# The first stage of a fused token, attention and mixture-of-experts kernel: order of loads, of the readout bias and of the first transposes, and which tokens a partition holds

## The chip, the cores and the metric

The kernel runs on one core of a Trainium2 chip. The metric is the device time of one execution in microseconds (us), the median of several runs. Everything is computed in float32; where a product needs precision on TensorE, each operand is split into a high and a low part (`_hi`, `_lo`, type fp32r) and three matmuls are added up.

## The reference, cut to what matters

```python
# x: 16 x 256 x 256 (batch, tokens, features); token 0 of each batch is the readout token
readout, other = X[:, :1, :], X[:, 1:, :]
h = gelu(other @ W[:d] + readout @ W[d:] + b)                    # token stage, exact gelu
def attn(x):                                                     # 16 heads of 64
    q, k, v = split(x @ Wq.T), split(x @ Wk.T), split(x @ Wv.T)
    e = exp(s - max(s)), s = q k^T / 8
    return merge(e / (sum(e) + 1e-10) @ v) @ Wo.T + bo
def moe(x):                                                      # 8 experts, best 2 per row
    routed = sum over the best two experts of p_e * (silu(x @ w1[e]) @ w2[e])
    shared = sigmoid(x @ gate_w) * ((silu(gate) * up) @ shared_down)
    return routed + shared
h = h + attn(layernorm(h))
h = h + moe(layernorm(h))                                        # out: 16 x 255 x 256
```

## The kernel before

The 4096 rows of x (16 batches of 256 tokens) are worked on in 8 groups of two batches, 512 rows each. A group lies in SBUF as 128 partitions by 4 row tiles (`GT` = 4) by 256 features; tile t of partition p is token p of the half-batch t. The result of the token stage, `resid`, keeps this layout to the end of the program, and the stores to `out` undo it.

The program has two blocks. Between them all engines meet at a barrier.

`token_phase` is the first block. For each group g, TensorE does in this order: the 12 matmuls of the token product into `tok_ps` (helper lines L70 to L72; `group`), the 8 transposes of the next group's input (`transpose_x`, L198, out to `xT_ps`), 8 transposes that prepare two banks of the attention weights (`weights`, L242), and the 8 transposes that turn the result back to rows (`rows`, L255, out to `h_ps`). ScalarE does four gelus (L287), then the high parts of the next input (`x_hi`, L275) and of the weights (L296). VectorE does the low parts (`x_lo`, L313; weights, L324) and then copies `h_ps` to `resid` (L328). After four groups VectorE has the layernorm statistics of the first group and GpSimd its reciprocal deviation; in group 5 VectorE writes the normalised rows `z` (L339).

Ahead of group 0 TensorE transposes the 16 readout rows (`ro`, L206), transposes the first input tile, and multiplies the readout rows by the lower half of the token weight (L213, the readout bias). VectorE copies the transposed readout rows (L301), splits the token weight (`tokw_lo`, L303), adds the bias column (`rbias`, L307), and only then makes the low parts of the first input tile (L313). ScalarE splits the token weight first (`tokw_hi`, L268) and then the input tile. All loads of this block are issued on SyncE's queue, in the order readout rows, token weight, two input tiles, the four attention weights, and then six more input tiles, each of which waits for the transposes that free its buffer.

`main_phase` is the second block: attention over the 8 groups with the router of the group before mixed in, then the expert tiles (71 of them), then the sums and the stores. Its first work on TensorE is `transpose_z` of group 0 (L676, out to `pT_ps`), on ScalarE a load of the exp table (L1032) and `z_hi` (L1057), on VectorE some constants, two pairs of statistics and `z_lo` (L1274); then come the first q and k projections (L70 to L72 into `proj_ps`). Every engine's order is written out by hand, and semaphores connect them. In `store_group` each group is stored by three DMAs (L615, L617, L619) once its last addition (L1470) is done.

Of the kernel before, what the change touches and what calls it, by code (L numbers as in the profile page):

```python
# [62 lines left out]
def f32(ap):  # L63

    return ap.bitcast(F32)
# [9 lines left out]
def build(nc, x, tok_w, tok_b, wq, wk, wv, wo, bo, router_w, w1, w2, gate_up, down, gate_w, out):  # L75
    x_rows = x.rearrange("b (h p) d -> p (b h) d", p=P)
    with ExitStack() as ctx:
# [15 lines left out]
                                                                  "rstd_ready", "z_ready")]  # L93
        qkv_at = nc.sbuf_base
# [4 lines left out]
        token_phase(nc, x, x_rows, tok_w, tok_b, wq, wk, wv, wo, resid, z, norm_sems, ident, half_neg,  # L99
                    qkv_parts, [wo_both[:, n] for n in range(2)])  # L100
        main_phase(nc, bo, router_w, gate_w, w1, w2, gate_up, down, out, resid, z, norm_sems, ident, half_neg,
# [3 lines left out]
def token_phase(nc, x, x_rows, tok_w, tok_b, wq, wk, wv, wo, resid, z, norm_sems, ident, half_neg,  # L105
                qkv_parts, wo_parts):


    with ExitStack() as ctx:
# [25 lines left out]
        s_ro, s_tokw, s_bcol = sem("ro_in"), sem("tokw_in"), sem("bcol_in")  # L135
# [14 lines left out]
        s_st, s_mv, s_var, s_rstd, s_z = norm_sems  # L150

# [50 lines left out]
        def _(pe):  # L202
            pe.wait_ge(s_const, IDENT_SET)
            pe.wait_ge(s_ro, 16)
# [3 lines left out]
            transpose_x(pe, 0)  # L208
            pe.wait_ge(s_readout, ROT_READY)
            pe.wait_ge(s_tokw, 16)  # L210
            for e in range(DC):
                for c in range(DC):
                    m = pe.matmul(h_ps[1][:, e * B:(e + 1) * B], tokw[:, DC + c, e * P:(e + 1) * P], roT[:, c, :],  # L213
                                  start=c == 0, stop=c == DC - 1)
            m.then_inc(s_readout, 1)

            def group(g, last):
# [6 lines left out]
                for e in range(DC):  # L224
# [4 lines left out]
                    m.then_inc(s_tok, 1)  # L229
                if not last:  # L230
                    transpose_x(pe, g + 1)

            def weights(g):

                for j in range(per_group):
# [7 lines left out]
                    m.then_inc(s_w, 1)  # L243

# [14 lines left out]
            for g in range(GROUPS):  # L259
                group(g, g == GROUPS - 1)  # L260
                weights(g)
                rows(g)

        @block.scalar
        def _(act):
            act.dma_start(bcol[:], tok_b.rearrange("(c p) -> p c", p=P), allow_slow_non_contiguous=True).then_inc(s_bcol, 16)
            act.wait_ge(s_tokw, 16)
            act.activation(tokw_hi[:], tokw[:, 0:DC, :], ACT.Copy).then_inc(s_tw, 1)  # L268

# [6 lines left out]

            x_hi(0)
            for g in range(GROUPS):
# [12 lines left out]
                for j in range(per_group):  # L291
# [7 lines left out]
        def _(dve):  # L299
            dve.wait_ge(s_readout, ROT_IN_PSUM)  # L300
            dve.tensor_copy(roT[:], h_ps[0][:, 0:DC * B].rearrange("p (c b) -> p c b", c=DC)).then_inc(s_readout, 1)  # L301
            dve.wait_ge(s_tw, TOKW_HI)
            dve.tensor_tensor(tokw_lo[:], tokw[:, 0:DC, :], f32(tokw_hi[:]), ALU.subtract).then_inc(s_tw, 1)  # L303
# [5 lines left out]

            def x_lo(g):  # L310
# [35 lines left out]
def main_phase(nc, bo, router_w, gate_w, w1, w2, gate_up, down, out, resid, z, norm_sems, ident, half_neg, qkv_parts,  # L346
# [11 lines left out]
    with ExitStack() as ctx:  # L358
# [308 lines left out]
        def _(pe):  # L667
# [252 lines left out]
            for c in range(DC):  # L920
                transpose_z(0, c)
# [939 lines left out]
```

## Time and profile before

| | us |
|---|---|
| median of 3 runs | 1057.47 (1057.09 to 1058.63) |
| the profiled execution's own time | 1057.78 |
| span of its profile | 1056.0 |
| PE busy | 1010.3 (96%) |
| DVE busy | 741.5 (70%) |
| ACT busy | 660.6 (63%) |
| POOL busy | 510.8 (48%) |

PE is TensorE's matmul side and PEld its weight loads, DVE is VectorE, ACT is ScalarE, POOL is GpSimd, SP is SyncE; a q behind the name (SPq) is the issue of DMAs. The span runs from the first to the last recorded instruction or transfer; 1.8 us of the execution lie outside it. PE's busy share is that of the whole span: it holds for the attention and the experts, and not for the first ten microseconds, the passage between the two blocks and the end.

### The profile page before, as it was taken

Reading aid. Unit: us, or ns where it says so; the run is one execution under the profiler, and the core shown is the slowest. Engines: PE = TensorE matmul, PEld = TensorE weight load, DVE = VectorE, ACT = ScalarE, POOL = GpSimd, SP = SyncE. Lnnn points to the kernel's source line nnn. Section 1 sums busy time; section 2 is a strip of 40 time slices with the busy share of each in tenths; the row PEclk is TensorE's granted clock in tenths of the full one; section 3 lists DMA queues with packets and bytes.
Section 4 is the critical chain, followed back from the end, with each engine's and each line's share of the span. In section 5 each row is a group of like instructions: output and inputs, shape, how many; then the busy total and the mean of one; then the engine's idle time right before and its main releaser. Section 6 shows DMA issues by size and latency. Waiting matters only on the chain.

```text
span 1056.0 us, 23175 instructions
## 1 busy us (share of the span) xinstructions
PE 1010.3 (96%) x8042; PEld 875.0 (83%) x8042; DVE 741.5 (70%) x1912; ACT 660.6 (63%) x1939; POOL 510.8 (48%) x557
## 2 busy tenths in 40 slices
PE   6979999999999999999999999999998889999996
PEld 5867888888888888888888888888876779998985
DVE  3757775787688578767857876775783766666677
ACT  4657884787578478757847775784783555554541
POOL 0016543557365455736645573664444486444420
PEclk9999999999999999999999999999999999999998
DMA  8210000001000000100000010000021834444479
GB/s 269 71 46 2 1 2 1 21 1 42 21 1 22 21 21 2 42 21 2 21 22 21 1 42 21 1 22 21 22 70 62 265 89 139 133 142 122 127 225 318
DMA packets 47496, 65.91 MB, mean 62 GB/s; under 512 B 7992, under 2 KB 39480, under 8 KB 47384
## 3 DMA queue, kind: packets, MB, share of 16 engines
q1 hardware_dynamic: 40056, 44.50, 13.5%
q0 software_dynamic: 7056, 19.93, 5.6%
q8 instruction: 68, 1.11, 0.4%
q14 instruction: 44, 0.36, 0.1%
q10 hardware_dynamic: 272, 0.00, 0.0%
HBM read 36.09 MB, written 28.33 MB: 61 GB/s over the span
## 4 chain that ended last, share of the span: by engine, by line
PE 73%; DVE 9%; DMA 4%; ACT 4%; issue 2%; SPq 2%; POOL 0%; DVEq 0%; ACTq 0%; POOLq 0%
PE proj_ps L70 12%; PE proj_ps L72 12%; PE proj_ps L71 12%; PE pT_ps L731 10%; PE proj_ps L744 10%; PE s_ps L713 8%; DMA back<-expert_out_rows 2%; ACT prob L1041 2%; DMA xg<-expert_in_rows 2%; PE s_ps L70 2%; PE s_ps L72 2%; PE s_ps L71 2%; PE s_ps L963 1%; PE pT_ps L984 1%; DVE z L1389 1%
## 5 line engine op out<-in xcount | busy, mean ns | idle before, releaser
L1041 ACT ACTIVATE prob<-s_ps,nmax 128x255 f32<-128x255 f32 x512 | 237.8, 479 | 140.5 <-DVE nmax L1263 139.5
L1720 POOL TENSOR_SCALAR prob<-prob,rinv 128x255 f32<-128x255 f32 x128 | 138.4, 1081 | 258.5 <-DVE rinv L1281 258.0
L1263 DVE TENSOR_REDUCE nmax<-s_ps 128x2 f32<-128x510 f32 x256 | 159.2, 679 | 23.2 <-PE s_ps L713 22.7
L731 PEld LDWEIGHTS pT_ps<-ident,prob 128*128 128x128 f32 x1024 | 114.6, 140 | 37.3 <-issue 29.1
L731 PE MATMUL pT_ps<-ident,prob 128*128 128x128 f32 x1024 | 136.9, 276 | 3.6 <-ACT probT L1067 3.3
L744 PE MATMUL proj_ps<-probT,v 128*64 128x256 f32 x1024 | 125.1, 386 | 2.1 <-DVE probT L1288 2.1
L1722 POOL TENSOR_SCALAR prob<-prob,rinv 128x255 f32<-128x255 f32 x128 | 119.2, 931 | 0.0
L1270 DVE TENSOR_TENSOR qk_space<-proj_ps,qk_space 128x512 fp32r<-128x512 f32 x128 | 87.6, 685 | 38.2 <-ACT qk_space L1053 37.8
L1048 ACT ACTIVATE prob<-prob,rinv 128x255 f32<-128x255 f32 x128 | 67.3, 526 | 66.7 <-DVE rinv L1281 66.5
L713 PE MATMUL s_ps<-qk_space 64*128 64x256 f32 x1536 | 108.3, 287 | 0.4 <-DVE qk_space L1270 0.3
L1041 ACT ACTIVATION_READ_ACCUMULATOR prob<-s_ps,nmax 128x1 f32 x512 | 108.5, 212 | 0.0
L713 PEld LDWEIGHTS s_ps<-qk_space 64*128 64x128 f32 x1536 | 95.3, 186 | 8.0 <-issue 2.3
L1811 POOL DMA_INDIRECT expert_out_rows<-yg,y_at x71 | 68.1, 959 | 68.3 <-DVE yg L1626 63.3
L744 PEld LDWEIGHTS proj_ps<-probT,v 128*64 128x64 f32 x1024 | 67.8, 136 | 38.8 <-issue 2.1
L1053 ACT ACTIVATE qk_space<-proj_ps 128x512 fp32r<-128x512 f32 x128 | 79.0, 618 | 14.8 <-PE proj_ps L72 14.6
L1288 DVE COPY probT<-pT_ps 128x512 f32<-128x512 f32 x128 | 87.0, 679 | 0.0
L70 PE MATMUL proj_ps<-wv_hi,zT_lo 128*128 128x256 f32 x256 | 77.6, 303 | 2.3 <-DVE qk_space L1270 2.2
L1067 ACT ACTIVATE probT<-pT_ps 128x512 f32<-128x512 f32 x128 | 79.0, 618 | 0.8 <-PE pT_ps L731 0.8
L1744 POOL DMA_INDIRECT expert_in_rows<-z,slot_now x64 | 64.3, 1005 | 25.5 <-issue 17.4
L1293 DVE TENSOR_TENSOR oT_lo<-proj_ps,oT_hi 128x512 fp32r<-128x512 f32 x64 | 44.2, 691 | 45.8 <-ACT oT_hi L1072 45.8
L71 PE MATMUL proj_ps<-wo_both,oT_hi 128*128 128x256 f32 x256 | 72.5, 283 | 0.0
L70 PE MATMUL proj_ps<-wo_both,oT_lo 128*128 128x256 f32 x256 | 72.5, 283 | 0.0
(261 smaller groups left out, 2697.5 us busy)
## 6 DMA issues: line engine op xcount, KB each, us to landing
xg<-expert_in_rows SPq DMA_DIRECT2D x71, 130.0 KB
back<-expert_out_rows SPq DMA_DIRECT2D x6, 1024.0 KB, 21.6
xin<-in_x_dram SPq DMA_DIRECT2D x8, 512.0 KB, 4.6
z_rows<-z SPq DMA_DIRECT2D x8, 512.0 KB, 3.2
z<-z_rows SPq DMA_DIRECT2D x8, 512.0 KB, 4.4
expert_in_rows<-bo_row SPq DMA_DIRECT2D x16, 128.0 KB
raw_up<-in_L_ffn_w_dram SPq DMA_DIRECT2D x8, 256.0 KB, 5.4
raw_down<-in_L_ffn_w_dram SPq DMA_DIRECT2D x8, 256.0 KB, 6.1
```

Of the source, the lines that this page charges most:

```text
L70: pe.matmul(out, wl, xh, start=start, stop=False, skip_group_check=True)
L71: pe.matmul(out, wh, xl, start=False, stop=False, skip_group_check=True)
L72: return pe.matmul(out, wh, xh, start=False, stop=stop, skip_group_check=True)
L713: m = pe.matmul(s_ps[b][h][:, qt * N:(qt + 1) * N], a[part, rows], k[part, keys], start=n == 0, stop=n == 2)
L731: m = pe.transpose(pT_ps[h][:, o:o + P], prob[u_par(u)][:, h, qt, kt * P:(kt + 1) * P], ident[:])
L744: m = pe.matmul(o_ps[h * DH:(h + 1) * DH, b * N:(b + 1) * N], vt[:, 2 * b + kt, col:col + DH], probT[b][:, h, kt, :], start=kt == 0, stop= ...
L1041: m = act.activation(prob[u_par(u)][:, h, qt, 1:N], s_ps[b][h][:, qt * N + 1:(qt + 1) * N], ACT.Exp, bias=nmax[b][:, n:n + 1], accum_out=r ...
L1263: dve.tensor_reduce(nmax[b][:, 2 * h:2 * h + 2], s_ps[b][h][:].rearrange("p (q k) -> p q k", q=2)[:, :, 1:N], AX_X, ALU.max, negate=True). ...
L1270: dve.tensor_tensor(lo[:], proj_ps[j % 2][:], f32(hi[:]), ALU.subtract).then_inc(s_qkl, 1)
L1288: dve.tensor_copy(probT[i % 2][:, 1, :, :], pT_ps[1][:].rearrange("p (k q) -> p k q", k=2)).then_inc(s_pB, 1)
L1720: pool.tensor_scalar(prob[k][:, 0, 1, 1:N], prob[k][:, 0, 1, 1:N], rinv[k][:, 1:2], None, ALU.mult).then_inc(s_nA1, 1)
L1722: pool.tensor_scalar(prob[k][:, 1, 0, 1:N], prob[k][:, 1, 0, 1:N], rinv[k][:, 2:3], None, ALU.mult).then_inc(s_nB, 1)
```

## The change

Five things change, all in the first block but the last part of the fifth.

1. The first input tile is the first load on SyncE's queue, then come the readout rows, the token weight in two halves with a semaphore each, and the second input tile. The later input tiles stand between the attention weights, and each still waits for the transposes that free its buffer; the loads of wk, wv and wo now stand behind such waits.
2. TensorE transposes the first input tile before the readout rows, and multiplies for the readout bias after group 0's token product.
3. VectorE makes the low parts of the weight and of the first tile before it copies the readout rows and adds the bias.
4. The transposes of `z` for group 0 and the high and low parts of them are made at the end of the first block, by `transpose_z` in group 7 ahead of `rows`, into the banks of `xT_ps`; the second block begins with the projections.
5. Partition p holds the tokens 2p and 2p+1 of each batch in place of p and p+128. A load or store of a partition then touches runs of two rows (2 KB) in place of one (1 KB). The three stores of a group have other shapes: rows of partitions 16 to 127, of 1 to 15, and the one row (token 1) of partition 0.

```diff
-    x_rows = x.rearrange("b (h p) d -> p (b h) d", p=P)
+    x_rows = x.rearrange("b (p h) d -> p b (h d)", p=P)
@@ block.sync, first block
+            def load_x(g):
+                if g >= 2:
+                    sp.wait_ge(s_xT_ps, DC * (g - 1))
+                sp.dma_start(xin[g % 2][:].rearrange("p (b h) d -> p b (h d)", b=2),
+                             x_rows[:, 2 * g:2 * g + 2, :]).then_inc(x_in[g % 2], 16)
+
+            load_x(0)
             sp.dma_start(ro[:], x[:, 0, :]).then_inc(s_ro, 16)
-            sp.dma_start(tokw[:], tok_w.rearrange("(c p) e -> p c e", p=P)).then_inc(s_tokw, 16)
-            sp.dma_start(xin[0][:], x_rows[:, 0:GT, :]).then_inc(x_in[0], 16)
-            sp.dma_start(xin[1][:], x_rows[:, GT:2 * GT, :]).then_inc(x_in[1], 16)
+            for n in range(2):
+                sp.dma_start(tokw[:, n * DC:(n + 1) * DC, :],
+                             tok_w[n * D:(n + 1) * D, :].rearrange("(c p) e -> p c e", p=P)).then_inc(s_tokw[n], 16)
+            load_x(1)
             for i, w in enumerate((wq, wk, wv)):
                 sp.dma_start(raw[i][:], w.rearrange("(r p) d -> p r d", p=P)).then_inc(s_raw[i], 16)
+                load_x(2 + i)
             sp.dma_start(raw_o[:], wo.rearrange("(c p) i -> p c i", p=P)).then_inc(s_raw[3], 16)
-            for g in range(2, GROUPS):
-                sp.wait_ge(s_xT_ps, DC * (g - 1))
-                sp.dma_start(xin[g % 2][:], x_rows[:, GT * g:GT * g + GT, :]).then_inc(x_in[g % 2], 16)
+            for g in range(5, GROUPS):
+                load_x(g)
@@ block.tensor, in group(g, last)
+                if g == 0:
+                    readout_bias()
                 if not last:
                     transpose_x(pe, g + 1)
...
+            def transpose_z():
+                pe.wait_ge(s_z, GT)
+                for c in range(DC):
+                    for t in range(GT):
+                        m = pe.transpose(xT_ps[c][:, t * P:(t + 1) * P], z[:, t, c * P:(c + 1) * P], ident[:])
+                    m.then_inc(s_zt, 1)
...
                 weights(g)
+                if g == GROUPS - 1:
+                    transpose_z()
                 rows(g)
@@ block.scalar, at its end
+            for c in range(DC):
+                act.wait_ge(s_zt, c + 1)
+                act.activation(zT_hi[:, c, :], xT_ps[c][:], ACT.Copy).then_inc(s_zh, 1)
@@ block.vector, ahead of the copies of h_ps
+                if g == GROUPS - 1:
+                    for c in range(DC):
+                        dve.wait_ge(s_zh, c + 1)
+                        dve.tensor_tensor(zT_lo[:, c, :], xT_ps[c][:], f32(zT_hi[:, c, :]), ALU.subtract).then_inc(s_zl, 1)
@@ store_group, second block
-                rows = resid[:, GT * g:GT * g + GT, :].rearrange("p (b h) d -> p b h d", h=2)
-                sp.dma_start(out[2 * g:2 * g + 2, HEAD - 1:P - 1, :].rearrange("b p d -> p b d"),
-                             rows[HEAD:P, :, 0, :]).then_inc(s_out, 16)
-                sp.dma_start(out[2 * g:2 * g + 2, 0:HEAD - 1, :].rearrange("b p d -> p b d"),
-                             rows[1:HEAD, :, 0, :]).then_inc(s_out, 16)
-                sp.dma_start(out[2 * g:2 * g + 2, P - 1:N - 1, :].rearrange("b p d -> p b d"),
-                             rows[:, :, 1, :]).then_inc(s_out, 16)
+                rows = resid[:, GT * g:GT * g + GT, :].rearrange("p (b h) d -> p b (h d)", h=2)
+                both = out[2 * g:2 * g + 2, 1:N - 1, :].rearrange("b (p h) d -> p b (h d)", h=2)
+                sp.dma_start(both[HEAD - 1:P - 1], rows[HEAD:P]).then_inc(s_out, 16)
+                sp.dma_start(both[0:HEAD - 1], rows[1:HEAD]).then_inc(s_out, 16)
+                sp.dma_start(out[2 * g:2 * g + 2, 0:1, :].rearrange("b p d -> p b d"),
+                             rows[0:1, :, D:2 * D]).then_inc(s_out, 16)
@@ block.tensor, block.scalar and block.vector, second block: the first lines go
-            for c in range(DC):
-                transpose_z(0, c)
...
-            for c in range(DC):
-                z_hi(0, c)
...
-            for c in range(DC):
-                z_lo(0, c)
```

The next piece is TensorE's order at the start of the program, as a difference (line, operation, out<-in, shape, count).

```order
-L206 MATMUL h_ps<-ident,ro 128x16 x2
-L198 MATMUL xT_ps<-ident,xin 128x128 x8
-L213 MATMUL h_ps<-roT,tokw 128x16 x4
+L210 MATMUL xT_ps<-ident,xin 128x128 x8
+L219 MATMUL h_ps<-ident,ro 128x16 x2
 L70 MATMUL tok_ps<-xT_hi,tokw_lo 128x512
 L71 MATMUL tok_ps<-xT_lo,tokw_hi 128x512
```

The four bias matmuls (L213, now L227) have left their place ahead of the token product; they stand behind its twelfth matmul, ahead of the transposes of tile 1. VectorE's order at the same place, before:

```order
L301 COPY roT<-h_ps 128x32 [waits readout_bias_step]
L303 TENSOR_TENSOR tokw_lo<-tokw,tokw_hi 128x512 [waits tokw_step]
L307 TENSOR_SCALAR rbias<-h_ps,bcol 128x16 [waits bcol_in,readout_bias_step]
L307 TENSOR_SCALAR rbias<-h_ps,bcol 128x16
L313 TENSOR_TENSOR xT_lo<-xT_ps,xT_hi 128x512 [waits xT_hi_ready] x4
```

And of the change:

```order
L333 TENSOR_TENSOR tokw_lo<-tokw,tokw_hi 128x512 [waits tokw_step]
L330 TENSOR_TENSOR xT_lo<-xT_ps,xT_hi 128x512 [waits xT_hi_ready] x2
L336 COPY roT<-h_ps 128x32 [waits readout_bias_step]
L340 TENSOR_SCALAR rbias<-h_ps,bcol 128x16 [waits bcol_in,readout_bias_step]
L340 TENSOR_SCALAR rbias<-h_ps,bcol 128x16
L330 TENSOR_TENSOR xT_lo<-xT_ps,xT_hi 128x512 [waits xT_hi_ready] x2
```

The first tile's two low parts no longer stand behind the bias. VectorE's order across the end of the first block (L109 and L111 are the barrier), before:

```order
L324 SCALAR_TENSOR_TENSOR wo_both<-w_ps,wo_both 128x512 [waits w_hi_ready] x2
L328 COPY resid<-h_ps 128x512 [waits h_in_psum] x2
L109 UNCONDITIONAL_BRANCH
```

And of the change:

```order
L350 SCALAR_TENSOR_TENSOR wo_both<-w_ps,wo_both 128x512 [waits w_hi_ready] x2
L355 TENSOR_TENSOR zT_lo<-xT_ps,zT_hi 128x512 [waits zT_hi2] x2
L358 COPY resid<-h_ps 128x512 [waits h_in_psum] x2
L111 UNCONDITIONAL_BRANCH
```

The two low parts of `zT` have moved in front of the last two copies of the block; the same pair stood behind the statistics of the second block.

## Rows read from the trace of the kernel before

**Rows 1.** Stretches: us, busy time per engine, granted clock, DMA share, GB/s.

```profile
0.00:62.00 62.00, 50.79 (x298) 43.32 (x298) 34.12 (x64) 32.41 (x67) 2.00 (x9) 1.00 0.45 145
90.00:854.00 764.00, 753.06 (x6192) 639.04 (x6188) 558.18 (x1453) 519.88 (x1580) 406.85 (x439) 1.00 0.09 30
1012.00:1056.00 44.00, 34.29 (x197) 30.12 (x196) 33.96 (x50) 11.70 (x21) 3.62 (x4) 0.91 0.96 298
```

**Rows 2.** Timeline, first 13 us: start, us busy, engine, line, what, [idle before].

```profile
1.26 0.41 SPq L171 DMA_DIRECT2D tokw<-in_L_tok_W_dram  x1
1.72 0.50 SPq L172 DMA_DIRECT2D xin<-in_x_dram  x1
5.38 0.63 ACT L268 ACTIVATE tokw_hi<-tokw 128x512 fp32r<-128x512 f32 x1 [2.81 <-DMA tokw<-in_L_tok_W_dram]
6.88 1.97 PE L198 MATMUL xT_ps<-ident,xin 128*128 128x128 f32 x8 [3.97 <-DMA xin<-in_x_dram]
8.64 1.73 PE L213 MATMUL h_ps<-roT,tokw 128*128 128x16 f32 x8
8.89 0.60 ACT L275 ACTIVATE xT_hi<-xT_ps 128x512 fp32r<-128x512 f32 x1 [0.26 <-PE xT_ps L198]
10.41 0.38 DVE L307 TENSOR_SCALAR rbias<-h_ps,bcol 128x16 f32<-128x16 f32 x2 [3.68 <-PE h_ps L213]
10.70 1.28 DVE L313 TENSOR_TENSOR xT_lo<-xT_ps,xT_hi 128x512 fp32r<-128x512 f32 x2
12.04 0.80 PE L70 MATMUL tok_ps<-xT_hi,tokw_lo 128*128 128x512 f32 x1 [1.66 <-DVE xT_lo L313]
```

**Rows 3.** Timeline, group 0 to group 1, and group 7's first matmul.

```profile
15.05 1.28 ACT L287 ACT_TABLE_LOAD   x1 [5.57 <-PE tok_ps L72]
16.35 0.84 ACT L287 ACTIVATE hT<-tok_ps,rbias 128x256 f32<-128x256 f32 x2
16.90 0.49 PE L72 MATMUL tok_ps<-xT_hi,tokw_hi 128*128 128x512 f32 x1
17.42 0.84 ACT L287 ACTIVATE hT<-tok_ps,rbias 128x256 f32<-128x256 f32 x2 [0.24 <-PE tok_ps L72]
20.12 0.50 PE L70 MATMUL tok_ps<-xT_hi,tokw_lo 128*128 128x512 f32 x1
54.83 0.50 PE L70 MATMUL tok_ps<-xT_hi,tokw_lo 128*128 128x512 f32 x1
```

**Rows 4.** DMA issues: what, count, KB each, median us to landing.

```profile
raw_v<-in_L_attn_Wv_dram SPq DMA_DIRECT2D x1, 1024.0 KB, 11.9
tokw<-in_L_tok_W_dram SPq DMA_DIRECT2D x1, 512.0 KB, 4.1
```

**Rows 5.** Timeline, end of the first block and start of the second.

```profile
57.69 1.03 PE L242 MATMUL w_ps<-ident,raw_o 128*128 128x128 f32 x8
58.78 1.09 PE L255 MATMUL h_ps<-ident,hT 128*128 128x128 f32 x8
59.25 1.29 DVE L324 SCALAR_TENSOR_TENSOR wo_both<-w_ps,wo_both 128x512 fp32r<-128x512 f32 x2 [2.09 <-ACT wo_both L296]
60.45 1.28 DVE L328 COPY resid<-h_ps 128x512 f32<-128x512 f32 x2
62.20 1.06 PE L676 MATMUL pT_ps<-ident,z 128*128 128x128 f32 x8 [2.33 <-PEq L109]
64.09 1.29 DVE L1274 TENSOR_TENSOR zT_lo<-pT_ps,zT_hi 128x512 fp32r<-128x512 f32 x2 [0.52 <-ACT zT_hi L1057]
65.43 0.80 PE L70 MATMUL proj_ps<-zT_hi,wq_lo 128*128 128x512 f32 x1 [2.17 <-DVE zT_lo L1274]
```

**Rows 6.** One stretch after the barrier, columns as in rows 1.

```profile
64.00:66.00 2.00, 0.57 (x1) 0.50 (x2) 1.29 (x2) 0.54 (x2) 0.00 (x0) 0.72 0.25 34
```

**Rows 7.** Timeline, the last additions and the last store's issue.

```profile
1050.46 1.66 DVE L1470 SCALAR_TENSOR_TENSOR resid<-proj_ps,gates,resid 128x256 f32<-128x256 f32 x4
1053.10 0.39 SPq L619 DMA_DIRECT2D out_dram<-resid  x1
```

More of the change, by code:

```diff
@@ L93, in build @@
                                                                   "rstd_ready", "z_ready")]
+        zT = [ctx.enter_context(nc.sbuf_tensor(n, [P, DC, GR], F32R)) for n in ("zT_hi", "zT_lo")]
+        zT_sems = [ctx.enter_context(nc.semaphore(n)) for n in ("zT_in_psum", "zT_hi2", "zT_lo2")]
         qkv_at = nc.sbuf_base
@@ L207, in _, with readout_bias @@
             m.then_inc(s_readout, 1)
[L208 to L211, printed above, removed]
-                for c in range(DC):
-                    m = pe.matmul(h_ps[1][:, e * B:(e + 1) * B], tokw[:, DC + c, e * P:(e + 1) * P], roT[:, c, :],
-                                  start=c == 0, stop=c == DC - 1)
-            m.then_inc(s_readout, 1)
+            def readout_bias():
+                pe.wait_ge(s_readout, ROT_READY)
+                pe.wait_ge(s_tokw[1], 16)
+                for e in range(DC):
+                    for c in range(DC):
+                        m = pe.matmul(h_ps[1][:, e * B:(e + 1) * B], tokw[:, DC + c, e * P:(e + 1) * P], roT[:, c, :],
+                                      start=c == 0, stop=c == DC - 1)
+                m.then_inc(s_readout, 1)
             def group(g, last):
@@ L296, in _, with x_lo @@
                     act.activation(hi, src, ACT.Copy, scale=banks[n][3]).then_inc(s_w_hi, 1)
+            for c in range(DC):
+                act.wait_ge(s_zt, c + 1)
+                act.activation(zT_hi[:, c, :], xT_ps[c][:], ACT.Copy).then_inc(s_zh, 1)
         @block.vector
         def _(dve):
+            def x_lo(g):
+                for c in range(DC):
+                    dve.wait_ge(s_xT_hi, DC * g + c + 1)
+                    dve.tensor_tensor(xT_lo[:, c, :], xT_ps[c][:], f32(xT_hi[:, c, :]), ALU.subtract).then_inc(s_xT_lo, 1)
+            dve.wait_ge(s_tw, TOKW_HI)
+            dve.tensor_tensor(tokw_lo[:], tokw[:, 0:DC, :], f32(tokw_hi[:]), ALU.subtract).then_inc(s_tw, 1)
+            x_lo(0)
             dve.wait_ge(s_readout, ROT_IN_PSUM)
             dve.tensor_copy(roT[:], h_ps[0][:, 0:DC * B].rearrange("p (c b) -> p c b", c=DC)).then_inc(s_readout, 1)
-            dve.wait_ge(s_tw, TOKW_HI)
-            dve.tensor_tensor(tokw_lo[:], tokw[:, 0:DC, :], f32(tokw_hi[:]), ALU.subtract).then_inc(s_tw, 1)
             dve.wait_ge(s_readout, BIAS_IN_PSUM)
@@ L325, in _ @@
                                              op1=ALU.subtract).then_inc(s_w_lo, 1)
+                if g == GROUPS - 1:
+                    for c in range(DC):
+                        dve.wait_ge(s_zh, c + 1)
+                        dve.tensor_tensor(zT_lo[:, c, :], xT_ps[c][:], f32(zT_hi[:, c, :]), ALU.subtract).then_inc(s_zl, 1)
                 for j in range(2):
@@ L343, with main_phase @@
 SHARED_EARLY = 4
-def main_phase(nc, bo, router_w, gate_w, w1, w2, gate_up, down, out, resid, z, norm_sems, ident, half_neg, qkv_parts,
-               qkv_at, wo_both, wo_at, gates, tile_tables, z_dram, x_slots, y_rows):
+def main_phase(nc, bo, router_w, gate_w, w1, w2, gate_up, down, out, resid, z, norm_sems, zT, zT_sems, ident, half_neg,
+               qkv_parts, qkv_at, wo_both, wo_at, gates, tile_tables, z_dram, x_slots, y_rows):
     COLS = 16
@@ L372, in main_phase @@
         bo_row = sb("bo_row", [P, D])
-        zT_hi, zT_lo = (sb(n, [P, DC, GR], F32R) for n in ("zT_hi", "zT_lo"))
+        zT_hi, zT_lo = zT
         qk_space = sb("qk_space", [P, 8, GR], F32R)
```

25 lines of the change are left out of this document (11 added, 14 removed).

## The prediction

> **What bounds the kernel now.** I read the stretches first: they say where TensorE is the bound and where it stands idle. From 90 to 854 us it is busy 753.06 of 764 us, so a start that comes earlier by some time moves this whole stretch by that time. In the first 62 us it is busy 50.79, with VectorE at 34.12 and ScalarE at 32.41: there the order decides, not an engine's load. In the last 44 us the DMA engines are busy 96% and VectorE 33.96 us [rows 1]. So the change can pay at the start, at the barrier and at the very end, and nothing in between gets shorter. Next I read the timeline of the start and of the barrier, each time from the TensorE instruction that had idled back to what it waited for.
>
> At the start, the first input tile lands with the transposes at 6.88 and the token product begins only at 12.04; ahead of it stand the low parts, which began at 10.70, 0.4 us after the bias began [rows 2]. At the barrier, the last copies begin at 60.45, the transposes of z come at 62.20, their low parts at 64.09, and the projections at 65.43 [rows 5].
>
> **The clock.** Group 0 runs at the lower level, 1.2 GHz: eight transposes at 6.88 take 1.97 us against 1.06 at 62.20, and a matmul of 512 columns takes 0.80 us at 12.04 and at 65.43, against 0.50 at 20.12 [rows 2, 3, 5]. From 12.04 to 16.90 are eleven steps, 0.44 us each. The granted clock is 0.72 on average from 64 to 66 us [rows 6]. For the change I need when it rises. In group 0 it rose about 5 us after the product began, since the product's last matmul (0.49 us) is at the full level again [rows 3].
>
> **Term 1, the start.**
> - Input tile. Its issue moves from 1.72 to the first place, about 0.9 us earlier (the token weight, second in line, was issued at 1.26). The first large load in the trace lands 4.1 us after its issue [rows 2, 4]; at the same delay the tile is there at 0.8 + 4.1 = 4.9. Bounds: 5.95 with the tile's own old delay (6.88 - 1.72), and 2.6, were there nothing but 512 KB at 298 GB/s [rows 1]. I take 4.9; below 5.1 the tile doesn't decide, since the weight is later.
> - Token weight, lower half only (256 KB) behind the tile. Between the weight's use at 5.38 and the tile's at 6.88, 512 KB went by in 1.5 us; so 0.75 us for the half: 5.7. Bounds 5.38 and 6.88 [rows 2].
> - Both split. ScalarE: weight 5.7 to 6.35 (0.63), tile halves to 6.95 and 7.58 (0.60 each); the tile's second transposes are done by 4.9 + 2.0 = 6.9 and don't hold it. VectorE: weight low part to 7.05, tile low parts 1.28 for two, the second behind 7.58: done at 8.35. The product begins at 8.4 in place of 12.04: 3.6 us earlier.
> - What is late next: the first gelu. It needs the product's first half, a table load (1.28) and the bias. The table load started 3.0 after the product (15.05 - 12.04) and waits for the product alone: it ends at 8.4 + 3.0 + 1.3 = 12.7. The bias now stands behind the whole product: 8.4 + 4.86 + 0.43 = 13.7 for the product, then the bias matmuls. They took 1.73 at the low clock; at the full one 0.9 (by the ratio 1.06 to 1.97). With a rise 5 us after 8.4 they run at the full clock: 14.6, plus 0.45 for `rbias` and two hand-overs: the gelu at 15.1 in place of 16.35, 1.25 us earlier. The four gelus then need no pause (the pause at 17.42 was 0.23): group 1's product, at 20.12 before, comes 1.5 us earlier [rows 2, 3]. So of 3.6 us the bias takes back 2.1. Bounds: with bias at the low clock and the weight at 6.88 the gain is nothing; with the clock up right after the first half it is 2.7.
> - Groups 1 to 7 repeat with (54.83 - 20.12) / 6 = 5.8 us [rows 3], and nothing in them moves: 1.5 us stays.
> - Edits at nothing. wk now waits for the transposes of tile 0, wv for tile 1 (16 us), wo for tile 2 (about 21). The slowest of these loads takes 11.9 us [rows 4], so wv is there at 28 and wo at 33; they are used in groups 4 and 6, after 20.1 + 3 x 5.8 = 37 and 49. Behind the waiting issues on SyncE stand only later tiles that wait for the same transposes. Readout rows and their transposes have 6 us of slack. If that cover went, each microsecond of lateness would be one in the sum.
>
> **Term 2, the barrier.** Added in the first block: eight transposes (about 0.9 us of TensorE between 58.7 and 59.6; the last transposes then end near 60.6), two high parts on ScalarE, two low parts on VectorE. VectorE is the one that ends the block. It finishes the weights at 60.54, does the two low parts (1.29) and then the two copies (1.28, starting at 60.45 before): the copies end at 63.0 in place of 61.7. ScalarE's high parts are ready by about 60.4 and 61.0, in time. From the copies' end to TensorE's first instruction of the second block were 62.20 - 61.73 = 0.47 us; so the projections begin at 63.5 in place of 65.43: 1.95 us earlier [rows 5]. ScalarE loads the exp table at once after the barrier, about 1.5 us, and is first needed 3 us after the projections' start: covered. The stage that goes is 65.43 - 62.20 = 3.2 us. Bounds: 0.9, had the added transposes and low parts stood one behind the other on the path (3.2 - 1.29 - 1.06), and 3.2, had they cost nothing.
>
> At 63.5 TensorE has stood idle for 2.9 us. It stayed at the full clock over 2.33 us of idling before 62.20, and had fallen by 65.43. I assume it has fallen again, at 63.5 as at 65.43, so that the slow stretch just moves.
>
> A rule bears on this. The transposes at 62.20 ran at the full clock although since 57.69 TensorE had done nothing but transposes [rows 5]. The Trainium skill ("TensorE: Matmul & The Clock Gate", Part 4: PE-mode transpose) says that transposes don't count as activity for the clock. By it the clock would have been low at 62.20, and in the change the fall before 63.5 would be certain; the sum would be the same 1.95. The trace speaks against the rule here, and so leaves room for rival A.
>
> **Term 3, the stores.** VectorE ends at 1052.12 and the last of three stores is issued at 1053.10; the span ends 2.9 us later [rows 1, 7]. The last store was 256 KB (128 rows of each of two batches) and is now one row of each; the large one (448 KB) is now the first, issued some 0.9 us earlier but 192 KB larger, which at 298 GB/s is 0.65 us [rows 1]. Gain 0.9 - 0.65, about 0.2 us; bounds 0 and 0.9. Loads and stores in runs of 2 KB: the eight groups' stores are 8 x 0.51 = 4.1 MB, 14 us of full DMA at 298 GB/s. That any run length changes this rate the rows don't show; from VectorE's chain in the last part I take it as hidden, and give it to a rival.
>
> **Sum.** 1.5 + 1.95 + 0.2 = 3.65 us. The profiled execution took 1057.78 (span 1056.0), which becomes 1054.1; it stood 0.31 above the median of 1057.47, so the median becomes 1053.8.
>
> **The rivals.**
> - A, the clock is kind: it doesn't fall before 63.5, or rises soon after 8.4. Six matmuls from 65.43 on cost 0.44 in place of half of that, so 1.3 us more are won there; at the start up to 1.2 with the second half of the product. For it: idling of 2.33 us did not lower it. Against: 2.9 is longer, and it had fallen by 65.43. Time: 1053.8 - 1.3 - 0.6 = 1051.9.
> - B, the readout bias takes the place of the low parts: the bias matmuls run at the low clock (0.8 more) and the weight's half lands near 6.9 (up to 1.2 more). The start gains nothing: 1057.47 - 2.15 = 1055.3. For it: the weight is now third in line. Against: only 0.8 MB stand up to its end, where the old tile had 1.05.
> - C, the gain is absorbed: the expert tiles or the last sums wait for DMA anyway (96% share in the last 44 us), and what comes earlier waits longer there. Against: those loads are issued when their inputs are ready, so they move too. Time: 1056.9, no change.
> - D, slower: stores in runs of 2 KB go slower. Place: the last 44 us, DMA at 96%. Each 10% of rate lost costs 1.4 us of the 14; from 26% on the gain of 3.65 is eaten, and at half as slow again (7 us) the time is 1060.8. For it: DMA is full there. Against: half the runs for the same bytes, and nothing in the rows that grows with a run's length.
>
> **How the numbers follow.** Forecast 50% (its own range 1052.8 to 1054.8), A 20%, B 17%, C 8%, D 5%. Leaving out D, most of C and A's far end gives the range 1051.5 to 1056.0. A measurement of this kernel tells 0.2%, 2.1 us, from no change: faster is below 1055.4. Faster: forecast, A and over half of B, 81%. Within 0.2%: C and the rest of B, 15%. Slower: 4%.
>
> **What would show it.** Token product at 8.4 (right if 8 to 9); table load at 11.4; bias matmuls behind the product, then a pause of ScalarE for `rbias` ahead of the gelu; group 1's product at 18.6; the copies' end 1.3 later against group 7's product (54.83 to 61.73 before, 8.2 us after); first projection at 62.0 in the new time (65.43 - 3.45); all later stages 3.45 earlier. It is wrong if the first gelu is not earlier than 16, if the copies end over 9 us behind group 7's product, or if the lead at 90 us is not there at 1012.

## The result, and the profile after

| | before | after |
|---|---|---|
| median, us | 1057.47 (5 runs, 1054.96 to 1059.23) | 1050.57 (5 runs, 1048.97 to 1050.81) |
| ratio of the times | | 0.9938, 95% interval 0.9921 to 0.9954 |
| span of the profile | 1056.0 | 1048.8 |

By the ratio the change is faster by 6.6 us (0.62%). The forecast was 1053.8, range 1051.5 to 1056.0: the sign is right, the gain nearly twice as large, the time below the range. Four runs of those below took 1122 to 4371 us, far above all others of their kernels; they are in no mean and no ratio.

The stretches of the kernel after, 2.5 us and 7 us earlier than in [rows 1], columns as there:

```profile
0.00:62.00 62.00, 51.46 (x306) 43.74 (x306) 34.91 (x66) 33.16 (x69) 2.00 (x9) 1.00 0.44 145
87.50:851.50 764.00, 754.41 (x6193) 639.50 (x6189) 558.38 (x1453) 519.88 (x1580) 406.91 (x439) 1.00 0.09 30
1005.00:1049.00 44.00, 34.74 (x204) 30.50 (x202) 34.53 (x50) 11.98 (x21) 3.61 (x4) 0.93 0.92 298
```

They look as before, so the gain is in the parts between them. The timeline of the start, for [rows 2, 3]:

```profile
0.81 0.47 SPq L177 DMA_DIRECT2D xin<-in_x_dram  x1
5.70 1.94 PE L210 MATMUL xT_ps<-ident,xin 128*128 128x128 f32 x8 [5.70 <-DMA xin<-in_x_dram]
6.36 0.63 ACT L300 ACTIVATE tokw_hi<-tokw 128x512 fp32r<-128x512 f32 x1 [3.76 <-DMA tokw<-in_L_tok_W_dram]
7.63 1.37 DVE L330 TENSOR_TENSOR xT_lo<-xT_ps,xT_hi 128x512 fp32r<-128x512 f32 x2
9.05 0.80 PE L70 MATMUL tok_ps<-xT_hi,tokw_lo 128*128 128x512 f32 x1 [1.09 <-DVE xT_lo L330]
12.07 1.28 ACT L311 ACT_TABLE_LOAD   x1 [3.79 <-PE tok_ps L72]
14.34 1.36 PE L227 MATMUL h_ps<-roT,tokw 128*128 128x16 f32 x8
15.74 0.38 DVE L340 TENSOR_SCALAR rbias<-h_ps,bcol 128x16 f32<-128x16 f32 x2 [6.64 <-PE h_ps L227]
16.15 1.57 ACT L311 ACTIVATE hT<-tok_ps,rbias 128x256 f32<-128x256 f32 x4 [2.79 <-DVE rbias L340]
19.58 0.50 PE L70 MATMUL tok_ps<-xT_hi,tokw_lo 128*128 128x512 f32 x1 [0.72 <-DVE xT_lo L330]
```

The product starts 3.0 us earlier, but the gelus wait 2.79 us for `rbias`, and of the 3.0 us only 0.54 are left at group 1's product (19.58 for 20.12). The timeline of the barrier, for [rows 5], and after it the stretch for [rows 6]:

```profile
54.31 0.50 PE L70 MATMUL tok_ps<-xT_hi,tokw_lo 128*128 128x512 f32 x1
58.05 1.04 PE L265 MATMUL xT_ps<-ident,z 128*128 128x128 f32 x8
58.73 1.29 DVE L350 SCALAR_TENSOR_TENSOR wo_both<-w_ps,wo_both 128x512 fp32r<-128x512 f32 x2 [2.08 <-ACT wo_both L320]
58.92 1.04 PE L278 MATMUL h_ps<-ident,hT 128*128 128x128 f32 x8
59.05 1.10 ACT L323 ACTIVATE zT_hi<-xT_ps 128x512 fp32r<-128x512 f32 x2
59.94 1.28 DVE L355 TENSOR_TENSOR zT_lo<-xT_ps,zT_hi 128x512 fp32r<-128x512 f32 x2
61.13 1.28 DVE L358 COPY resid<-h_ps 128x512 f32<-128x512 f32 x2
62.91 0.73 PE L70 MATMUL proj_ps<-zT_hi,wq_lo 128*128 128x512 f32 x1 [2.95 <-PEq L111]
```

```profile
62.00:64.00 2.00, 1.09 (x3) 0.94 (x4) 1.43 (x8) 1.25 (x1) 1.22 (x8) 0.74 0.05 16
```

The copies end at 62.41, 8.10 after group 7's first matmul; the projections come 2.52 us earlier, 2.0 of them won here. The granted clock falls here too (0.74, before 0.72).

Where both profiles stand, by single rows of the two timelines:

| place | start before, after, us | gained since the row above |
|---|---|---|
| group 1's product | 20.12, 19.58 | 0.54 |
| first projection | 65.43, 62.91 | 1.98 |
| first load of an expert tile's rows | 854.72, 851.74 | 0.46 |
| transposes of the first tile's hidden rows | 864.77, 860.31 | 1.48 |
| first load of `back` | 1012.18, 1005.89 | 1.83 |
| end of the span | 1056.0, 1048.8 | 0.91 |

Of the 7.2 us by which the two profiles differ, 4.2 come behind 854 us, in a part of which the diff touches only the stores at its very end. The stretches of its beginning and of its tiles, before:

```profile
856.00:860.00 4.00, 2.22 (x18) 1.75 (x17) 2.76 (x9) 1.83 (x5) 4.00 (x4) 1.00 0.45 123
860.00:864.00 4.00, 4.00 (x24) 4.00 (x23) 0.46 (x2) 0.38 (x1) 4.00 (x5) 0.57 0.27 71
864.00:1004.00 140.00, 135.24 (x1118) 130.85 (x1117) 91.27 (x280) 73.07 (x209) 74.15 (x75) 1.00 0.42 126
```

and after:

```profile
856.00:860.00 4.00, 3.32 (x28) 3.33 (x29) 1.15 (x4) 0.38 (x1) 4.00 (x4) 1.00 0.39 103
860.00:998.00 138.00, 134.96 (x1116) 130.80 (x1115) 90.83 (x279) 73.29 (x209) 75.75 (x78) 1.00 0.42 128
```

Before, the granted clock fell to 0.57 on average over four of those microseconds, behind idling; after, it didn't. That is no property of the two kernels: of the eighteen profiles, five have this fall at the first tiles (before, e4, e10, e11, e13), one of them with the change in it. There one of the first intervals between tiles is 5.4 us, in the thirteen others at most 4.0. So about 1.5 of the 7.2 us are luck of these two profiles. The tiles hold the same work (1118 and 1116 matmuls, 135 us) in 140 and in 138 us. What the longest idle times in them are, the chain of waits of before shows (start, us, link):

```profile
944.99 0.49 DVE yg L1626
945.50 0.27 SPq L600
945.80 0.15 SPq L600
946.22 3.26 DMA xg<-expert_in_rows
...
955.33 0.49 DVE yg L1626
955.85 0.27 SPq L600
956.17 0.15 SPq L600
956.54 0.34 issue
956.88 4.26 DMA xg<-expert_in_rows
```

Tile n's rows are loaded into the buffer that tile n-6 frees. In before TensorE uses them 2.8 us (median) after the load's issue, and a tile takes 1.88 us. Most loads are well within that; the change has

```profile
DMA to landing us min/median/max: 2.0/2.1/2.8
```

from issue to landing, where the profile has all of a load's events. The two in the chain took 3.26 and 4.26 us: it is such slow ones that come late. Call excess the time by which the intervals between the 71 tiles exceed 1.88 us, over the intervals longer than 2.0: 8.3 us before, 6.4 after. TensorE's recorded waits for these loads are a part of it: 2.9 us before, 1.1 after.

### The profile page after: what moved, and what is told of

The parts are those of the page before. It is cut to its first block, busy times and chain, and to the rows that moved or that the text cites. A ratio compares the mean times of both kernels' runs of the same rounds, so it can differ in the third digit from the quotient of the medians.

```text
span 1048.8 us, 23176 instructions
## 1 busy us (share of the span) xinstructions
PE 1009.4 (96%) x8042; PEld 873.5 (83%) x8042; DVE 741.3 (71%) x1912; ACT 660.2 (63%) x1939; POOL 510.8 (49%) x557
## 4 chain that ended last, share of the span: by engine, by line
PE 75%; DVE 10%; ACT 3%; DMA 3%; issue 2%; POOL 0%; SPq 0%; DVEq 0%; ACTq 0%; POOLq 0%
PE proj_ps L70 12%; PE proj_ps L72 12%; PE proj_ps L71 12%; PE pT_ps L760 10%; PE proj_ps L773 10%; PE s_ps L742 9%; ACT prob L1068 2%; PE s_ps L70 2%; DMA back<-expert_out_rows 2%; PE s_ps L72 2%; PE s_ps L71 2%; PE pT_ps L1011 2%; PE s_ps L990 1%; DVE z L1414 1%; DVE probT L1313 1%
```

## The experiments

Means over all runs tell small differences better than medians of five, so they stand here together (before: 80 runs, in the four sets in which the other kernels were run; the change: 11 runs in two sets). The sets differ: before alone has 1057.48, 1056.94, 1058.25 and 1056.85 in them, so a difference of two means from different sets is known to about 1 us and no better. The ratios below are to the runs of before in the same set.

| kernel | mean us (runs) | granted clock, mean |
|---|---|---|
| before | 1057.24 (80) | 0.9913 |
| rows per partition alone (e1) | 1057.71 (12) | 0.9908 |
| z's transposes moved alone (e2) | 1053.22 (7) | 0.9943 |
| new start alone (e3) | 1055.24 (12) | 0.9912 |
| start and z (e4, e11) | 1052.12 (12) | 0.9941 |
| z and rows (e15) | 1054.40 (12) | 0.9936 |
| start and rows (e16) | 1054.53 (12) | 0.9916 |
| all three: the change | 1050.80 (11) | 0.9942 |

Averaging each part over the four pairs that differ in it alone: start -2.5 us, z -3.5, rows -0.1, each to about 0.6 either way. Added up they give 1051.4 for the change, 0.6 from what it has. One pair of parts may hang together: with the old start the new rows cost 0.5 and 1.2 us, with the new start they gain 0.7 and 1.3, and so the new start is worth 3.4 us with the new rows and 1.6 with the old. The difference, 1.8, is known to about 1.3 and rests on different sets; it is neither shown nor ruled out.

**e1, rows per partition alone.**

```diff
-    x_rows = x.rearrange("b (h p) d -> p (b h) d", p=P)
+    x_rows = x.rearrange("b (p h) d -> p b (h d)", p=P)
```

(and the loads and stores to it.) 

> The kernel before with the row layout of the change alone (a partition holds tokens 2p and 2p+1, loads and stores in runs of 2 KB); order of loads, bias and z transposes as before. The changed kernel is 6.9 us faster, of which its trace shows 2.6 before the expert tiles, 3.7 over them and about 0.8 behind them. Theory S (the layout acts only on the stores, and what the expert tiles gain is a changed meeting of their loads with the rest, not owed to the layout): 0.5 to 1.2 us faster than before, span of the expert tiles (first xg issue to first back issue, 157.5 us before) unchanged within its scatter. Theory L (the layout, by the order in which rows come to the experts or by its shorter DMA queues, shortens the expert tiles too): 3.5 to 5 us faster, the expert tiles at 154 us.

Measured: 1057.7, ratio 1.0 (0.9984 to 1.0015). The rows alone bring nothing and cost nothing, to about 1.6 us; neither theory's time came, and rival D is gone. In the profiles the stretch from the first load of `back` to the end is 43.3 us on average in eleven kernels with the new rows and 44.0 in seven with the old, so 0.7 us may be there.

**e2, z's transposes alone.**

```diff
+                if g == GROUPS - 1:
+                    transpose_z()
                 rows(g)
```

(and z's high and low parts with it, start as before.) 

> The kernel before with only group 0's z transposes, high and low parts moved into the first block. By the forecast's second term and the trace of the change (copies end 1.3 later, projections begin 1.9 to 2.0 earlier): 1.9 to 2.0 us faster in both theories if the rest of the program just moves; up to 5 us faster if a start earlier by any amount also helps the expert tiles (theory E).

Measured: 1053.58, ratio 0.9957 (0.994 to 0.9973). Its profile has the projections at 63.75 with 0.47 us for the first, at the full clock: the transposes' move pays what the forecast gave it and, in this execution, the fall of the clock too. By the ratio the kernel is 4.5 us faster (2.9 to 6.3), between the two expectations; 1.95 and the clock's 1.3 leave over 1 us of it unexplained.

**e3, the new start alone.**

```diff
+            load_x(0)
             sp.dma_start(ro[:], x[:, 0, :]).then_inc(s_ro, 16)
@@ in group(g, last), behind the product
+                if g == 0:
+                    readout_bias()
```

> The kernel before with only the new order of loads and of the readout bias, old row layout. By the trace of the change: token product of group 0 about 3.0 us earlier, first gelu only 0.2 earlier since it waits for the bias, group 1's product about 0.5 earlier; 0.5 us faster in total. The forecast had 1.5.

Measured: 1054.77, ratio 0.998 (0.9965 to 0.9994). Product at 9.09, gelu at 16.23, group 1's product at 19.67: the bias takes the gain back, as in the change. But the kernel is 2.1 us faster by the ratio (0.6 to 3.7), where 0.5 was expected: the rows at its own place don't account for it.

**e4, the change with the old rows per partition.**

```diff
-    x_rows = x.rearrange("b (p h) d -> p b (h d)", p=P)
+    x_rows = x.rearrange("b (h p) d -> p (b h) d", p=P)
```

> The change with the old row layout put back (tokens p and p+128, runs of 1 KB); start order and z transposes of the change. Theory S: 2.5 to 3 us faster than before, that is 4 slower than the change only if something else is at work, else within 1.2 of it. Theory L: 2.5 us faster than before, 4 to 4.5 slower than the change. Theory E (any earlier start helps the expert tiles): 6 us faster than before, within 1 us of the change.

**e5, the change again, unaltered.** 

> The changed kernel unaltered, for more runs beside the same runs of before. All theories: 1050 to 1051 us, mean granted clock about 0.994 against 0.991 of before.

Measured: e4 1050.96, ratio 0.9933 (0.9912 to 0.9954); e5 1051.04, ratio 0.9947 (0.9926 to 0.9967). No difference by the medians, so the rows aren't needed for most of the gain; by the means (1052.12 for e4 and e11, 1050.80) the rows are worth 1.3 us here and nothing in e1. e4's excess at the tiles is 7.7 us, e5's 6.6.

**e6, before with TensorE kept busy at the barrier.**

```diff
+            for n in range(9):
+                pe.matmul(tok_ps[n % 2][:], tokw_hi[:, 0, 0:P], xT_hi[:, 0, :], start=True, stop=True)
@@ second block, behind the transposes of z
+            for n in range(9):
+                pe.matmul(s_ps[0][n % 2][:], wq_hi[:, 0, 0:P], wq_hi[:, 0, 0:GR], start=True, stop=True)
```

> The kernel before with nothing moved; TensorE only gets matmuls without use (results never read) in its two idle stretches around the barrier, nine after the last transposes of the first block and nine behind the z transposes of the second. Theory clock (beyond the 2 us of the removed stage, moving z pays by keeping TensorE's clock up, since before it idles twice there and falls to 1.2 GHz for 3.4 to 6.8 us): the matmuls of the first q projection at 0.50 us in place of 0.80, mean clock from 0.991 to 0.994 or more, 2 to 3 us faster than before. Rival (an earlier start is worth more downstream, by the expert tiles): no low stretch at 65 us either, but the time changes by the 1.3 to 2.6 us that the projections win at most in the trace, and the expert stage keeps its length; if the time doesn't change at all, the clock there is not what paid.

Measured: 1055.87, ratio 0.999 (0.9975 to 1.0005); mean 1055.90, 1.3 below the mean of before and 1.0 below that of its own set. By its ratio it is not clear of noise, and the 2 to 3 us of the theory of the clock didn't come. Its timeline and stretches:

```profile
62.57 1.06 PE L679 MATMUL pT_ps<-ident,z 128*128 128x128 f32 x8 [0.45 <-PEq L109]
63.39 2.31 PE L926 MATMUL s_ps<-wq_hi 128*128 128x512 f32 x9
64.46 1.29 DVE L1279 TENSOR_TENSOR zT_lo<-pT_ps,zT_hi 128x512 fp32r<-128x512 f32 x2 [0.52 <-ACT zT_hi L1062]
65.80 0.50 PE L70 MATMUL proj_ps<-zT_hi,wq_lo 128*128 128x512 f32 x1
```

```profile
64.00:66.00 2.00, 1.90 (x9) 1.26 (x8) 1.29 (x2) 0.91 (x2) 0.09 (x1) 1.00 0.28 40
66.00:68.00 2.00, 2.00 (x10) 1.61 (x10) 0.00 (x0) 0.44 (x1) 0.00 (x0) 1.00 0.46 138
```

Before, the second of these stretches is

```profile
66.00:68.00 2.00, 2.00 (x6) 1.59 (x5) 0.00 (x0) 0.00 (x0) 0.00 (x0) 0.50 0.51 147
```

Six matmuls at 1.2 GHz against ten at 2.4: without idling the clock stays up, and in these two profiles the fall costs 1.3 us (122.61 from the projections to the first issue of `z_rows` before, 121.35 here).

**e7, the change with the first nine of these matmuls.** 

> The change plus nine matmuls without use behind the last transposes of the first block, which bridge most of the 2.9 us that TensorE idles there. Theory clock: no fall at the projections, mean clock 0.995 to 0.997, 1 to 2 us faster than the change. Rival: within 0.5 us of the change.

Measured: 1049.98, ratio 0.9933 (0.9911 to 0.9955); projections at 62.71, full clock, 121.37 us to `z_rows`. The mean, 1049.85, is 1.0 below the change (1.4 below e5, which ran in the same set): as expected, the fall of the clock that the change's profile shows is worth about that, and is to be had by not idling.

**e8, the readout bias in the middle of group 0's product.**

```diff
-                if g == 0:
-                    readout_bias()
+                    if g == 0 and e == 0:
+                        readout_bias()
```

> The change with the readout bias multiplied between the two halves of group 0's product in place of behind it. In the trace of the change the gelu waited for the bias from 13.35 (end of the table load) to 16.15. Theory: the first gelu at about 14.2, group 1's product 1.2 to 1.5 us earlier than in the change, the kernel 1.2 to 1.5 us faster. Rival (the first gelu is not what group 1 waits for): no difference to the change.

Measured: 1050.22, ratio 0.9936 (0.9914 to 0.9957). Its timeline:

```profile
11.78 1.72 PE L227 MATMUL h_ps<-roT,tokw 128*128 128x16 f32 x8
13.95 0.84 ACT L311 ACTIVATE hT<-tok_ps,rbias 128x256 f32<-128x256 f32 x2 [0.60 <-DVE rbias L340]
16.28 0.84 ACT L311 ACTIVATE hT<-tok_ps,rbias 128x256 f32<-128x256 f32 x2 [1.50 <-PE tok_ps L72]
19.05 0.49 PE L70 MATMUL tok_ps<-xT_hi,tokw_lo 128*128 128x512 f32 x1
```

The first gelus come 2.2 us earlier, then the second wait for the product's delayed half; 0.53 us is left at group 1's product, and 0.6 in the mean (1050.16; 1.1 beside e5). That is below the expected 1.2 to 1.5. Of the theory that the bias alone holds the start back, a part is right: moving it pays, but not all that it frees. The bias matmuls take 1.72 us in their new place, and the product's second half is at the lower level to its end.

**e9 and e10, seven buffers for the expert tiles' rows, in before and in the change.**

```diff
-    BUFS = 6
+    BUFS = 7
```

> The kernel before with seven buffers for the expert tiles' input in place of six, so that each load is issued one tile (1.9 us) earlier. In the profiles so far TensorE loses 7.4 to 8.3 us to intervals above 2.0 us between tiles in the kernels without the full change, and 4.9 to 7.0 us in those with it; part of it is waits for these loads (2.9 us of TensorE in the profile of before, 1.1 in that of the change). Theory X (the expert stage is shorter in the change since its loads come late less often): this one gains 2 to 3 us on before. Rival (the two differ in the expert stage by something else, such as the weight loads' fetches or chance): under 1 us.

> The change with seven such buffers. Theory X: it gains less here, 1 to 1.5 us on the change, so that the difference of the two kernels falls from 6.4 to about 5. Rival: the difference stays at 6.4.

Measured: e9 1050.98, ratio 0.9937 (0.992 to 0.9954); e10 1047.39, ratio 0.9903 (0.9886 to 0.9921). Both gain more than expected (2 to 3 us, and 1 to 1.5). The excess falls to 2.9 and 3.0 us, and TensorE waits 0.2 us and not at all for a tile's load. The tiles of e10:

```profile
859.00:993.50 134.50, 132.54 (x1116) 130.39 (x1115) 90.44 (x278) 72.79 (x209) 74.11 (x76) 1.00 0.43 131
```

The same 1116 matmuls in 134.5 us. By the means, the seventh buffer gives before 5.9 us and the change 3.2, and the two kernels now differ by 3.75 (1051.38, 1047.63, of one set; to about 1.5) in place of 6.4. About as much as the forecast's sum: most of the surplus hangs on the loads of these rows. The 5.9 us are twice the 2.9 that TensorE is seen to wait for them in before, so how a late load costs its whole price isn't shown row by row; a part can be the fall of the clock at the first tiles, which e9's profile doesn't have.

**e11, as e4, on another chip.** 

> The change with the old row layout once more, for more runs: so far 1051.9 (6 runs, mean) against 1050.8 of the change (11 runs) and 1057.3 of before. If the layout pays only in the stores' stage (0.65 us less from the first load of expert results to the end in five profiles against five), this stays 0.5 to 1 us behind the change; if the layout is worth nothing, within 0.3.

Measured: 1051.3, ratio 0.994 (0.9919 to 0.9961); excess 8.0. The mean of e4 and e11 (1052.12) carries the table's row.

**e12, the change with e7's nine matmuls, e8's bias and seven buffers.** 

> The change with all three: readout bias between the halves of the product (0.65 us in the means so far), nine filling matmuls at the barrier (0.96), seven input buffers (1 to 1.5 by theory X). By the sum 2.6 to 3.1 us faster than the change, 1047.7 to 1048.2; if the parts don't add (the gain ends in another wait), 1049.5.

Measured: 1046.21, ratio 0.9881 (0.9862 to 0.99); mean 1045.80, 11.4 us below before and 5.0 below the change, and 2 below what the expectation added up.

**e13 to e16, what makes the tiles wait less in the change.** e13 is before with the new rows and with

```diff
+        zT = [ctx.enter_context(nc.sbuf_tensor(n, [P, DC, GR], F32R)) for n in ("zT_hi", "zT_lo")]
```

declared ahead, so that the buffers lie where they do in the change; e14 is the change with

```diff
+            for n in range(14):
+                pe.matmul(s_ps[0][n % 2][:], wq_hi[:, 0, 0:P], wq_hi[:, 0, 0:GR], start=True, stop=True)
```

ahead of the first projection; e15 is e1 and e2 together, e16 e1 and e3.

> Before, with the new rows per partition and with the storage of zT declared ahead, so that every SBUF buffer of the second block lies at the address it has in the change; the order of work is that of before. If the addresses (with the rows) make the expert tiles' loads come in time: excess of the tiles' intervals about 5 to 6.5 us in place of 7.4 to 8.3, and the median 1055.5. If they do nothing: excess about 8, median 1057.5, as for the rows alone.

> The change, with 14 matmuls (128x512, result unused) on TensorE between the barrier and the first projection: the second block's first projection starts about 3.1 us later, at the full clock. If the experts' shorter waits hang on the time at which that stage starts: excess of the tiles' intervals back to about 8 us, and the median is the change's 1050.8 + 3.1 - 1.3 (clock) + 2 = 1054.6. If they hang on the change's layout or addresses: excess 5 to 7 us, median 1052.6.

> Before with the transposes of z moved into the first block and the new rows per partition, start of the program as before. If rows and addresses together carry the 2 us of the expert tiles: excess 5 to 6.5, last 44 us about 0.65 us shorter, median 1051.6. If it takes the start too: excess about 8, median 1053.2, as with the z move alone (1053.22 mean).

> The new start and the new rows per partition, transposes of z in the second block as before. If only the rows plus the start are wanted: excess 5 to 6.5, median 1053.3. If not: excess about 8, median 1055.0, as with the start alone (mean 1055.24).

Measured: e13 1057.94, ratio 1.0012 (0.9997 to 1.0027), excess 6.1; e14 1052.85, ratio 0.9964 (0.9946 to 0.9981), mean 1052.63, excess 4.6; e15 1054.06, ratio 0.9975 (0.9962 to 0.9988), excess 10.1; e16 1054.65, ratio 0.9977 (0.9965 to 0.9989), excess 8.0.

Addresses with the new rows give no time: e13's one profile has a smaller excess than before's, its twelve runs have none of the gain. e15 refutes that rows and the z move together carry it. A later start of the second block gives no excess back: in e14 the first projection is 4.3 us later than in the change and the tiles' first load 3.0 (854.71), the mean is 1.8 higher, and the excess is the smallest of all with six buffers; so the time at which the tiles begin isn't it. TensorE's two rows in e14:

```profile
62.45 4.95 PE L950 MATMUL s_ps<-wq_hi 128*128 128x512 f32 x14 [2.92 <-PEq L111]
67.24 0.39 PE L70 MATMUL proj_ps<-zT_hi,wq_lo 128*128 128x512 f32 x1
```

With six buffers, one profile each, the excess is 4.6 to 7.0 in the five of the change and its variants and 6.1 to 10.1 in the ten others: the two groups overlap. Only two kernels have two profiles each, and there it repeats within 0.3: 6.4 and 6.6 in the change, 7.7 and 8.0 without the new rows. So the excess may well be lower in the change, and why it should be stays open.

e16 holds what settles the start. Its start is that of the change, instruction for instruction, yet:

```profile
9.11 0.79 PE L70 MATMUL tok_ps<-xT_hi,tokw_lo 128*128 128x512 f32 x1 [1.29 <-DVE xT_lo L315]
12.68 0.52 PE L72 MATMUL tok_ps<-xT_hi,tokw_hi 128*128 128x512 f32 x1
13.04 0.40 PE L70 MATMUL tok_ps<-xT_hi,tokw_lo 128*128 128x512 f32 x1
13.75 0.96 PE L224 MATMUL h_ps<-roT,tokw 128*128 128x16 f32 x8
15.15 1.57 ACT L299 ACTIVATE hT<-tok_ps,rbias 128x256 f32<-128x256 f32 x4 [1.75 <-DVE rbias L325]
18.59 0.50 PE L70 MATMUL tok_ps<-xT_hi,tokw_lo 128*128 128x512 f32 x1 [0.72 <-DVE xT_lo L315]
```

The matmuls are at their full pace from 12.9 on, 3.8 us after the product began; in the profile of the change that came at 15.2, in the midst of the bias matmuls. The bias takes 0.96 us, and gelu and group 1's product stand at the forecast's 15.1 and 18.6.

## Why the prediction was wrong

**Term 1, the start: 1.5 forecast, 0.54 in the profile, 1.0 on average.** Group 1's product stands at 20.17 on average in the seven profiles with the old start and at 19.13 in the nine with the new (e8 and e12, with the bias elsewhere, aside). The loads were mis-sized. The input tile took 4.9 us from issue to use in place of 4.1 (5.70 for 4.9), and the weight's half was used at 6.36 in place of 5.7, so the product began at 9.05 and not 8.4. ScalarE goes from the weight to the tile with hardly a pause and waits only 0.20 us for the tile's second half: some 0.45 of the 0.65 us are the weight's, 0.2 the tile's. The rise of the clock was taken at 5 us after the product's start, from one row. In the sixteen profiles other than e8 and e12 it comes 3.3 to 6.2 us after, in the nine with the new start 5.0 on average, so the value was right; the profile of the change, with 6.1, is a late one, and there the bias matmuls take 1.36 us against 0.96 or 0.97 in six of the nine. The steps themselves held: table load 3.0 after the product, bias behind the product, ScalarE waiting for `rbias`. "The first gelu is not earlier than 16" was named as what would refute the term, and it came at 16.15 (in four of the nine profiles behind 16, in five ahead of it); rival B describes that profile better than the forecast.

**Term 2, the barrier: 1.95 forecast, 1.98 in the profile.** Added low parts, copies' end 8.10 behind group 7's product (8.2 forecast), first projection as worked out. But "the slow stretch just moves" holds in some executions only. In the profile of the change it does; of the eight profiles with the transposes moved and no added matmuls, the first projection is at the full clock in four (e2, e8, e10, e15), of the six with the transposes in the second block in none. The mean time from projection to `z_rows` is 122.1 us against 123.1, so rival A's first half is worth 1.0 us on average, not 1.3 always. The mean granted clock of whole runs agrees: 0.9936 and above where the transposes are moved, 0.9920 and below where they are not and no matmuls are added. It should have been a half-weighted term of the sum: that the clock falls where the transposes stand in the second block (six of six) doesn't say that it falls without them. The prediction had also weighed the Trainium skill ("TensorE: Matmul & The Clock Gate", Part 4: PE-mode transpose), by which transposes don't count as activity and the fall ahead of the projections would be certain. The runs speak against it: in e2, e8, e10 and e15 eight transposes each of weights, of z and of `hT`, and then 2.9 us of idling, preceded projections at the full clock.

**Term 3, the stores: 0.2 forecast.** From the last additions to the end of the span before 5.54 us (1050.46 [rows 7] to 1056.0), after 5.43:

```profile
1043.37 1.66 DVE L1495 SCALAR_TENSOR_TENSOR resid<-proj_ps,gates,resid 128x256 f32<-128x256 f32 x4
```

0.1 us, near the forecast. The other 0.8 of the last part comes ahead of the additions, and by e1 little of it is lasting.

**The step that failed** is in the first part: "nothing in between gets shorter". It rested on 90 to 854 us, where it is true ([rows 1]; lead 2.5 us at the projections, 2.6 at 743 us), and was carried on to 1012, a stretch of which no row was read. There 3.3 us came. Nearly half (1.5) is a fall of the clock that of these two profiles only before has, luck as five of the eighteen have it; the rest, 1.8, comes among the tiles, where TensorE's waits for their rows fell from 2.9 to 1.1 us. By the means, which such luck hardly moves, the surplus over the forecast is 6.4 - 3.65 = 2.8 us. Rival C looked at this place and had the sign wrong: it asked whether the gain is absorbed in waits, not whether the waits are stable. e9 and e10 show that a seventh buffer for these rows is worth 5.9 us to before and 3.2 to the change, and that with it the kernels differ by 3.75, near the forecast's 3.65. A second step failed beside it, "so that the slow stretch just moves": it put at nothing what is worth 1.0 us on average. What is left open is why the change makes fewer of these loads late: 1.5 of the start's 2.5 us and 0.6 of z's 3.5 are not explained by rows at their own places.

## What to carry to other kernels

Read every stretch of the span before saying that one doesn't move; where an engine waits for loads issued less than two tiles ahead (2.8 us for a load of 2.1 at the median and over 4 at times), a buffer more is worth looking at before any change of order elsewhere (here 5.9 us for one digit). A level of the clock seen in one profile is a draw: behind some 3 us of idling, put its cost in by halves or fill the gap with matmuls. Before moving a small product (here the readout bias) behind a large one, ask at which clock level it will run and who waits for it.

## What was not expected of the hardware

- The column of the granted clock reads 1.00 in the whole of group 0, while the matmuls follow each other at 0.43 us and later at 0.23. At the start only the durations show that TensorE is at 1.2 GHz and not at 2.4: the trace's first record of the clock is at 17.09 us before and at 15.17 after, and the column counts time without a record as full. From before:

```profile
12.00:13.00 1.00, 0.96 (x2) 0.83 (x3) 0.00 (x0) 0.00 (x0) 0.00 (x0) 1.00 1.10 347
```

- With the same instructions up to there and nearly the same start of the product (9.05 in the change, 9.11 in e16), that level ended some 2 us apart (15.2, 12.9).
- Idling of 2.9 us ahead of the projections lowered the clock in four of eight profiles (first projection 0.73 to 0.77 us against 0.47).
- Loads of 130 KB that land 2.1 us after issue at the median take 3.3 and 4.3 us now and then, and one buffer more was worth 5.9 us of 1057.
- Runs of 2 KB in place of 1 KB in loads and stores made no difference (1057.71 and 1057.24 in the mean).
